# Attention, FFN and two layer norms on one core: whole value groups, four single output transposes, and a longer lag in the FFN pipeline

## The reference

```python
N, S, D, H = 4, 2048, 512, 16
q, k, v = heads(x @ Wq.T), heads(x @ Wk.T), heads(x @ Wv.T)      # 16 heads of 32
attn = softmax(q @ k.T / sqrt(32)) @ v
x = layernorm(x + attn)
w = (weights >= 0) * 2 - 1
x = layernorm(x + clip((x @ w.T) * scale + bias, -100, 100))
```

## Time and profile before

| | |
|---|---|
| median of 3 runs | 2738.47 us (2737.49 to 2738.65) |
| time of the profiled execution | 2738.42 us |
| its span, first to last instruction | 2736.6 us |
| PE busy | 2690.3 us, 98% |
| ACT busy | 2277.5 us, 83% |
| DVE busy | 2214.1 us, 81% |
| POOL busy | 613.0 us, 22% |

### The profile page before, as it was taken

The page is one execution under the profiler, slowest core; times in us unless marked ns, Lnnn a source line. Parts: engine busy times, 40 slices in busy tenths (PEclk is TensorE's granted clock), DMA queues, the critical chain, the costliest instruction groups (busy, mean ns, idle before and its releaser), DMA issues. The chain is left out here.

```text
span 2736.6 us, 92216 instructions
## 1 busy us (share of the span) xinstructions
PE 2690.3 (98%) x38720; PEld 1722.2 (63%) x38720; DVE 2214.1 (81%) x2687; ACT 2277.5 (83%) x2726; POOL 613.0 (22%) x663
## 2 busy tenths in 40 slices
PE   9999999999999999999999999999999999996998
PEld 7888888755555555555555555555555555555776
DVE  7443333489999999989999999998999999986887
ACT  5333333399999999999999999999999999984665
POOL 1000000022222222222222222222222222224665
PEclk9999999999999999999999999999999999998999
DMA  6555555589898999989899998989999898976664
GB/s 232 193 194 185 184 186 193 192 173 194 173 200 175 197 181 194 194 167 204 172 202 183 187 198 167 209 170 200 185 180 201 173 204 170 190 144 189 208 209 135
DMA packets 311610, 512.33 MB, mean 187 GB/s; under 512 B 20930, under 2 KB 201154, under 8 KB 309060
## 3 DMA queue, kind: packets, MB, share of 16 engines
q0 software_dynamic: 73440, 267.42, 52.7%
q1 hardware_dynamic: 228004, 221.56, 26.1%
q10 hardware_dynamic: 9792, 17.83, 1.8%
HBM read 121.90 MB, written 117.44 MB: 87 GB/s over the span
## 5 line engine op out<-in xcount | busy, mean ns | idle before, releaser
L812 ACT ACTIVATE probs<-banks 128x1024 f32<-128x1024 f32 x2048 | 1896.7, 1073 | 11.7 <-PE banks L642 5.4
L642 PE MATMUL banks<-score_rows 97*32 97x512 f16 x16384 | 1269.6, 380 | 4.0 <-issue 3.9
L674 PE MATMUL banks<-probs,v_keys 128*32 128x256 f32 x16384 | 1268.4, 379 | 0.0
L674 PEld LDWEIGHTS banks<-probs,v_keys 128*32 128x32 f32 x16384 | 539.6, 110 | 377.7 <-issue 0.9
L614 POOL DMA_DIRECT2D total<-partial x510 | 440.1, 863 | 1465.6 <-DVE partial L902 675.7
L902 DVE TENSOR_TENSOR partial<-partial,probs 128x1024 f32<-128x1024 f32 x640 | 749.4, 1213 | 0.0
L642 PEld LDWEIGHTS banks<-score_rows 97*32 97x32 f16 x16384 | 463.2, 96 | 344.5 <-ACT probs L812 17.4
L898 DVE TENSOR_TENSOR partial<-probs 128x1024 f32<-128x1024 f32 x512 | 603.5, 1220 | 67.8 <-issue 55.8
L356 DVE TENSOR_TENSOR qk_lo<-banks,qk_hi 128x512 f16<-128x512 f32 x128 | 88.4, 690 | 241.2 <-ACT qk_hi L311 241.1
L311 ACT ACTIVATE qk_hi<-banks 128x512 f16<-128x512 f32 x128 | 76.0, 594 | 184.7 <-PE banks L228 184.7
L228 PE MATMUL banks<-xT_hi,w_hi 128*128 128x512 f32 x512 | 197.3, 389 | 0.0
(11 more groups left out here) (95 smaller groups left out, 2220.3 us busy)
## 6 DMA issues: line engine op xcount, KB each, us to landing
total<-partial POOLq DMA_DIRECT2D x510, 512.0 KB, 6.0
scratch_q_raw<-qk_raw SPq DMA_DIRECT2D x16, 1024.0 KB, 5.7
scratch_k_raw<-qk_raw SPq DMA_DIRECT2D x16, 1024.0 KB, 5.7
scratch_v<-v_out SPq DMA_DIRECT2D x16, 1024.0 KB, 5.2
score_rows<-scratch_q_hi SPq DMA_DIRECT2D x128, 128.0 KB, 5.3
score_rows<-scratch_k_hi SPq DMA_DIRECT2D x128, 128.0 KB, 5.5
v_keys<-scratch_v SPq DMA_DIRECT2D x64, 256.0 KB, 7.1
scratch_attn<-wf_scaled SPq DMA_DIRECT2D x64, 256.0 KB, 5.4
```

What stands on the lines that cost most here:

```text
L642: last = nc.tensor.matmul(scores_of(phase, unit)[part, i, :], k_rows[:, h, keys], q_rows[:, h, qb * BLK:(qb + 1) * BLK], start=True, stop= ...
L674: last = nc.tensor.matmul(banks[rows, out_bank(qb), cols], v_keys[:, kt, rows], probs[:, kt % P_RING, h, cols], start=(kt == 0 and part == ...
L812: nc.scalar.activation(probs[:, kt % P_RING, heads, :], scores_of(it % SLOTS, qb * UNITS + u), ACT.Exp, scale=SCALE / GAIN ** 2).then_inc( ...
```

## The change

Scores and values are no longer interleaved by halves: for each key tile PE issues both score units, and then the values of all four heads over the whole 512 queries, so the value matmuls are half as many and twice as wide. The four output transposes are no longer issued together after tile 4 but one each after tiles 3, 4, 5 and 6, each with its own increment of `a_turn`; DVE reads the turned output after tile 7 and not 5. The denominator pieces move from tiles 8 to 11 to tiles 9 to 12, their copy from after DVE's tile 12 to 13, their transpose from tile 13 to 14; DVE still inverts after tile 14. In the FFN pipeline the lags of TRANS, FFN, CLIP and LN2 each grow by one step.

```diff
-DEN_TILES = (8, 9, 10, 11)
-TURN_TILE = 4
-DEN_TURN_TILE = 13
-OUT_AFTER, TURNED_AFTER, DEN_AFTER, INVERT_AFTER, NORMAL_AFTER = 2, 5, 12, 14, 15
+DEN_TILES = (9, 10, 11, 12)
+TURN_TILES = (3, 4, 5, 6)
+DEN_TURN_TILE = 14
+OUT_AFTER, TURNED_AFTER, DEN_AFTER, INVERT_AFTER, NORMAL_AFTER = 2, 7, 13, 14, 15
...
-        def values(it, qb, kt, part):
+        def values(it, qb, kt):
...
             for h in range(G):
                 rows = slice(HD * h, HD * h + HD)
-                last = nc.tensor.matmul(banks[rows, out_bank(qb), cols], v_keys[:, kt, rows], probs[:, kt % P_RING, h, cols],
-                                        start=(kt == 0 and part == 0), stop=(kt == KT - 1), skip_group_check=True)
-            if part == 1:
-                last.then_inc(a_pv, 1)
+                last = nc.tensor.matmul(banks[rows, out_bank(qb), :], v_keys[:, kt, rows], probs[:, kt % P_RING, h, :],
+                                        start=(kt == 0), stop=(kt == KT - 1))
+            last.then_inc(a_pv, 1)
...
-        def turn_output(it, qb):
+        def turn_output(it, qb, c):
...
-            pe.wait_ge(a_out, st + 1)
-            for c in range(TPB):
-                cols = slice(c * P, (c + 1) * P)
-                last = nc.tensor.transpose(banks[:, out_bank(qb), cols], out_sb[:, cols], ident2[:])
-            last.then_inc(a_turn, 1)
+            if c == 0:
+                pe.wait_ge(a_out, it * QB + qb + 1)
+            cols = slice(c * P, (c + 1) * P)
+            nc.tensor.transpose(banks[:, out_bank(qb), cols], out_sb[:, cols], ident2[:]).then_inc(a_turn, 1)
...
-            if kt == TURN_TILE:
-                turn_output(it, qb)
+            if kt in TURN_TILES:
+                turn_output(it, qb, TURN_TILES.index(kt))
...
             for kt in tiles:
-                for half in range(2):
-                    if kt + LAG < KT:
-                        scores(it, phase, qb, kt + LAG, (half,))
-                    elif qb < QB - 1:
-                        scores(it, phase, qb + 1, kt + LAG - KT, (half,))
-                    elif it is not LAST:
-                        scores(it + 1, phase + 1, 0, kt + LAG - KT, (half,))
-                    values(it, qb, kt, half)
+                if kt + LAG < KT:
+                    scores(it, phase, qb, kt + LAG)
+                elif qb < QB - 1:
+                    scores(it, phase, qb + 1, kt + LAG - KT)
+                elif it is not LAST:
+                    scores(it + 1, phase + 1, 0, kt + LAG - KT)
+                values(it, qb, kt)
...
-    ATTN, LN1, TRANS, FFN, CLIP, LN2 = 0, 1, 2, 4, 5, 6
+    ATTN, LN1, TRANS, FFN, CLIP, LN2 = 0, 1, 3, 5, 6, 7
```

More of the change, by code:

```diff
@@ L470, in attend @@
     LAST = ITEMS - 1
-    HEAD = max(TURN_TILE, DEN_TURN_TILE, *DEN_TILES) + 1
+    HEAD = max(DEN_TURN_TILE, *TURN_TILES, *DEN_TILES) + 1
     FIRST_Q = 48
@@ L626, in _, with fast_scores @@
         pe.sem_inc(a_den, 2 * len(DEN_TILES))
-        def fast_scores(it, phase, qb, kt, halves=(0, 1)):
-            if kt == 0 and halves[0] == 0:
+        def fast_scores(it, phase, qb, kt):
+            if kt == 0:
                 pe.wait_ge(a_q[qb], it * FIRST_Q + FIRST_Q)
-            if qb == 0 and kt % TPB == 0 and halves[0] == 0:
+            if qb == 0 and kt % TPB == 0:
                 pe.wait_ge(a_k[kt // TPB], it * FIRST_K + FIRST_K)
-            for half in halves:
+            for half in range(2):
                 unit = qb * UNITS + 2 * kt + half
@@ L644, in fast_scores, with exact_scores @@
                 last.then_inc(a_score, 1)
-        def exact_scores(it, phase, qb, kt, halves=(0, 1)):
+        def exact_scores(it, phase, qb, kt):
             st = it * QB + qb
-            if kt == 0 and halves[0] == 0:
+            if kt == 0:
                 pe.wait_ge(m_q, st * 32 + 32)
-            if kt % TPB == 0 and halves[0] == 0:
+            if kt % TPB == 0:
                 pe.wait_ge(m_k[kt // TPB % 2], (st * QB // 2 + kt // TPB // 2) * 16 + 16)
             keys = slice(kt % (2 * TPB) * P, (kt % (2 * TPB) + 1) * P)
-            for half in halves:
+            for half in range(2):
                 unit = qb * UNITS + 2 * kt + half
@@ L660, in exact_scores @@
                 last.then_inc(a_score, 1)
-        def values(it, qb, kt, part):
+        def values(it, qb, kt):
             st = it * QB + qb
[L665 to L671, removed]
+            if qb == 0 and kt % TPB == 0:
+                pe.wait_ge(a_v[kt // TPB], it * 16 + 16)
+            pe.wait_ge(a_prob, st * UNITS + 2 * kt + 2 + SLOTS)
+            if kt == 0:
+                pe.wait_ge(a_dout, st + 1)
             for h in range(G):
                 rows = slice(HD * h, HD * h + HD)
-                last = nc.tensor.matmul(banks[rows, out_bank(qb), cols], v_keys[:, kt, rows], probs[:, kt % P_RING, h, cols],
-                                        start=(kt == 0 and part == 0), stop=(kt == KT - 1), skip_group_check=True)
-            if part == 1:
-                last.then_inc(a_pv, 1)
-        def turn_output(it, qb):
-            st = it * QB + qb
-            pe.wait_ge(a_out, st + 1)
-            for c in range(TPB):
-                cols = slice(c * P, (c + 1) * P)
-                last = nc.tensor.transpose(banks[:, out_bank(qb), cols], out_sb[:, cols], ident2[:])
-            last.then_inc(a_turn, 1)
+                last = nc.tensor.matmul(banks[rows, out_bank(qb), :], v_keys[:, kt, rows], probs[:, kt % P_RING, h, :],
[6 more added lines that the diff above has]
+            nc.tensor.transpose(banks[:, out_bank(qb), cols], out_sb[:, cols], ident2[:]).then_inc(a_turn, 1)
         def denominators(it, qb, piece):
@@ L748, in item @@
             else:
-                turn_output(it, QB - 1)
+                for c in range(TPB):
+                    turn_output(it, QB - 1, c)
                 for piece in range(TPB):
@@ L839, in copy_out @@
             dve.wait_ge(a_pv, st * KT + KT + P_RING)
-            dve.wait_ge(a_turn, st)
+            dve.wait_ge(a_turn, st * TPB)
             nc.vector.tensor_copy(out_sb, banks[:, out_bank(parity), :]).then_inc(a_out, 1)
         def copy_turned(st, parity):
-            dve.wait_ge(a_turn, st + 1)
+            dve.wait_ge(a_turn, (st + 1) * TPB)
             dve.wait_ge(a_norm, st)
```

## The result

The changed kernel takes 2764.59 us, the median of 4 runs (2763.99 to 2766.1), against 2738.56 us for the kernel before. The ratio is 1.0095 with a 95% interval of 1.0078 to 1.0113: 26 us slower, where 32 were forecast. The profiled execution took 2765.11 us, 1.9 over its span of 2763.2.

The account below looks back on a forecast made before the run. PE's gapless list was taken to bound attention (29.74 us a block, ACT's floor 29.33), a dependency loop the FFN. 2738.4 - 7 (whole groups) + 49 (output turns) - 10 (FFN) = 2770 us; range 2755 to 2790 for 8 in 10.

Parts of the forecast that it names:

- Four output turns: PE in attention: four lone transposes at 0.37 us replace one visit of 0.70, 0.78 us more per block, 49 us slower.
- Whole groups: PE's values in attention: rounds per key tile fall from four to two, saving 3.4 ns each, 7 us less.
- Score slots: ACT reads paired score units in 2.01 us, under the 2.17 available: no cost, by 0.1 us; otherwise 6 us.
- The denominators' turn unchanged: PE in attention: the full-width transpose of the denominators still costs 0.42 us, 0.05 of it from strips out of step.
- DVE's dates: DVE in attention: the output copy is ready 0.36 us before the first output turn needs it, so no cost.
- FFN: Last stage: y is needed two steps later, so the step falls from 3.776 to 3.67 us, 10 us gained.
- cheap lone transposes: Rival on output turns: each lone transpose costs only 0.11 us, 16 us less in attention, total 2705; chance 0.06.
- The late copy: Rival: DVE's output copy comes late, PE stands 0.5 us more per block, 31 us, total 2802; chance 0.10.
- The FFN without a gain: Rival in the last stage: another wait takes over or the extra step is paid for, 2781 to 2785; chance 0.12.
- the new visits are hidden: Rival in attention: PE's new visits fall into time it would have waited anyway, -7 - 10 or about no change; chance 0.03.

Follow-up runs that it names:

- six tiles: Changed kernel with output turns together after tile 4 and the denominators' turn on strips after tile 14, six tiles ahead of them: 2708.36 us, ratio 0.9890.
- seven: Changed kernel with output turns together after tile 4 and the old denominator tiles and FFN lags, leaving only whole value groups: 2734.82 us, ratio 0.9987.
- halves in pairs: Kernel before with only the order changed: scores of both halves, then both 256-query halves of the values: 2738.05 us, no difference.
- the output turns on strips: Changed kernel with each of its four lone output transposes made by four ordinary matmuls on strips of 32 columns: 2730.06 us, ratio 0.9972.
- two visits: Version with whole groups and longer FFN lags, output transposes made two after tile 4 and two after tile 5, copy after tile 7: 2740.54 us.

## Why the prediction was right

The mechanism and its order of size were right: attention loses by the lone transposes, the FFN gains by the lag. Of the terms of the sum:

- *Four output turns, +49.* Shown. 0.37 us each in the trace after; +46 us alone, where 0.05 us a block, 3 us, came back at the denominators' turn.
- *Whole groups, -7.* In size right for the changed kernel (8 ns a tile, 8 us); alone it gave 4, since PE then waits for ACT.
- *Score slots, nothing, by 0.1 us.* Right for the change, and near its edge: with six tiles the wait was 0.02 to 0.03, with seven 0.12.
- *The denominators' turn unchanged.* This is the mis-sized term. It went from 0.42 to 0.37, 3 us in all. I had put its 0.05 to strips out of step after the narrow pieces. That they were out of step is shown: the record of the values ahead is 0.65 us long at the denominators' turn of the kernel before and 0.60 at its output turn, 0.61 with lone turns alone (more in the last section). But the pieces alone don't make it. They stand in every version, and the 0.05 was gone (0.37 to 0.38 us) in the changed kernel, with whole groups alone, with lone turns alone, with halves in pairs and with the output turns on strips. Why the strips drift in the order of the kernel before, and in no other order that was run, is left open.
- *DVE's dates, nothing.* Shown, with the 0.36 us to spare.
- *FFN, -10.* 9.4 in the trace after, 10.6 alone. The step is DVE's own list, as said.

One us more from the whole groups, 3 from the denominators' turn and 0.6 less from the FFN make 3 to 4 of the 5 us between 2770 and 2764.6. The rest, under a tenth of a per cent, I can't place.

One inference was wrong without harm. I had read from the weight loads' even 0.41 us of idle time that a visit's price hardly varies. That idle time is the length of the group ahead (0.84 us with wide values), and the price of the denominators' turn did vary, as the last section shows.

Of the rivals, cheap lone transposes fell in the trace after, with lone turns alone and with two visits. The late copy was real as a danger, 0.36 us away, and did not happen. The FFN without a gain fell. That the new visits are hidden fell with 2784.77 us for them alone.

## What to carry to other kernels

When matmuls run on 32-column strips, a full-width operation between them has a fixed price beside its own, here 0.26 us for a transpose: do such operations together, or do them on strips as well (0.22 us against 0.37). When the engine that bounds has a list without gaps, add up that list from starts in the timeline, and the second engine's list beside it: the difference, here 0.41 us a block, is all that thinning out the first can bring. And ask how long the stretches without an insertion are, for there the second engine falls behind and fills the slots.

## What the runs showed of the hardware beside that

Strips can run out of step, and a full-width operation pays for it. In one block of the kernel before, a record of a denominator piece starts late, and PE's timeline goes on so:

```profile
2329.63 0.63 PE L674 MATMUL banks<-probs,v_keys 128*32 128x256 f32 x8
...
2330.37 0.27 PE L705 MATMUL banks<-total,select 128*32 128x128 f32 x1
...
2333.32 0.79 PE L674 MATMUL banks<-probs,v_keys 128*32 128x256 f32 x8
2334.03 0.33 PE L713 MATMUL banks<-ident,den_sb 128*128 128x128 f32 x1
2334.29 0.61 PE L642 MATMUL banks<-score_rows 97*32 97x512 f16 x8
```

Groups are 0.79 us long from there on and no longer 0.63, though they still start 0.434 apart: the last strip's records start some 0.15 us behind the others' and stay behind, at no cost to the stream. The turn then starts 0.71 us after the values and the scores 0.97 after them, where it is 0.58 and 0.84 in the block of the earlier trace rows; behind it groups are 0.61 long again. The lag cost nothing until the full-width transpose, which waited for the last strip and put them in step.

In a steady run ACT's starts are 0.90 us apart and its ends 0.917, while its records grow from 1.02 to 1.17 us; it was the ends that gave the floor of 29.33 us. The costs beside streaming depend on what stands next to what: four rounds of scores in a pair take 0.864 us, 2.7 ns each over their 0.2133. The Trainium skill, TensorE: Matmul & The Clock Gate, section Wait — 56ns, not 53.3ns?, has some 2.5 ns per matmul on top of its columns, and the trace is near this. The wide values' rounds take 0.431 us, 4 ns over twice 0.2133.
